# A two-layer attention and feed-forward kernel: the first attention turns its row maxima in two halves of query tiles, and its first step moves its queries in halves

## The reference, cut to what matters

```python
q = _rmsnorm(x @ wq_a.T, q_a_ln_w) @ wq_b.T          # per head 64 plain and 64 rotated columns
ckv, k_pe = split(x @ wkv_a.T)                        # latent of 32, shared rotated key of 64
k_nope, v = split(_rmsnorm(ckv, kv_a_ln_w) @ wkv_b.T)
q_pe, k_pe = _apply_rope(...), _apply_rope(...)       # x * cos + rotate_half(x) * sin
scores = einsum('bqhd,bkhd->bhqk', q_full, k_full) * softmax_scale
scores = where(causal, scores, lowest)
attn = softmax(scores, axis=-1)
out = einsum('bhqk,bkhd->bqhd', attn, v) @ wo.T
```

## Time and profile before

| what | us |
|---|---|
| median of 3 runs (2199.75 to 2222.36) | 2202.95 |
| the profiled execution, its own time | 2218.44 |
| the profiled execution, its span | 2216.7 |
| TensorE busy, share of the span | 2008.4, 91% |
| VectorE, ScalarE, GpSimd busy | 1167.0, 883.8, 480.9 |
| mean granted TensorE clock | 0.933 of full |

### The profile page before, as it was taken

The page is one execution under the profiler, slowest core; times in us unless marked ns, Lnnn a source line. Parts: engine busy times, 40 slices in busy tenths (PEclk is TensorE's granted clock), DMA queues, the critical chain, the costliest instruction groups (busy, mean ns, idle before and its releaser), DMA issues. The chain is left out here.

```text
span 2216.7 us, 34036 instructions
## 1 busy us (share of the span) xinstructions
PE 2008.4 (91%) x12632; PEld 1153.7 (52%) x12632; DVE 1167.0 (53%) x2541; ACT 883.8 (40%) x1861; POOL 480.9 (22%) x376
## 2 busy tenths in 40 slices
PE   5858999999999999999976899996999999999698
PEld 4535666656666656665643454553444444444244
DVE  3536555565555555556401454445676676673166
ACT  3402444444444444444430122221566665665222
POOL 0011444444443434444330000000000000000000
PEclk8867999999999999999997999995899999998699
DMA  9742232222333233322208221126132122211201
GB/s 310 254 136 58 58 78 57 58 60 70 78 78 78 68 78 78 78 55 55 67 23 258 67 67 52 51 93 138 21 51 46 34 49 47 37 30 22 92 29 48
DMA packets 100856, 172.19 MB, mean 78 GB/s; under 512 B 25738, under 2 KB 46378, under 8 KB 100562
## 3 DMA queue, kind: packets, MB, share of 16 engines
q1 hardware_dynamic: 100690, 170.01, 29.2%
HBM read 84.32 MB, written 29.38 MB: 51 GB/s over the span
## 5 line engine op out<-in xcount | busy, mean ns | idle before, releaser
L822 ACT ACTIVATE at_prob<-at_scp 128x512 f32<-128x512 f32 (+1 forms) x608 | 349.6, 575 | 533.1 <-PE at_scp L923 524.5
L856 DVE CUSTOM_DVE_ANT_0 at_junk<-at_mxp,causal 128x128 f32<-128x128 f32 (+3 forms) x512 | 240.5, 486 | 339.6 <-PE at_mxp L932 334.9
L1549 ACT ACTIVATE as_prob<-as_scp 128x512 f32<-128x512 f32 (+2 forms) x640 | 309.6, 563 | 202.2 <-PE as_scp L1645 149.5
L932 PE MATMUL at_mxp<-l_khi,at_qhi 96*128 96x512 f32 (+2 forms) x768 | 262.4, 406 | 24.9 <-DMA at_qhi<-at_shi 21.1
L919 PE MATMUL at_scp<-at_qhi,l_khi 97*128 97x512 f32 (+1 forms) x608 | 260.4, 428 | 8.2 <-issue 4.5
L1599 DVE TENSOR_REDUCE as_mxd<-as_mxp 128x2 f32<-128x256 f32 (+3 forms) x256 | 203.6, 821 | 105.3 <-PE as_mxp L1664 103.4
L922 PE MATMUL at_scp<-at_qlo,l_khi 96*128 96x512 f32 (+1 forms) x608 | 235.0, 387 | 0.0
L923 PE MATMUL at_scp<-at_qhi,l_klo 96*128 96x512 f32 (+1 forms) x608 | 233.6, 384 | 0.0
L1584 POOL TENSOR_TENSOR l_att_t<-l_att_t,as_spread 64x1024 f32<-64x1024 f32 x16 | 37.9, 2368 | 878.9 <-DMA as_spread<-l_recips 878.9
L1642 PE MATMUL as_scp<-as_q,l_keys 49*128 49x512 f32 (+2 forms) x640 | 213.9, 459 | 13.4 <-ACT as_prob L1549 10.8
L1659 PE MATMUL as_mxp<-l_keys,as_q 48*128 48x512 f32 (+2 forms) x768 | 186.9, 467 | 35.7 <-DVE as_mxf L1597 13.9
(11 more groups left out here) (204 smaller groups left out, 2742.1 us busy)
## 6 DMA issues: line engine op xcount, KB each, us to landing
at_qhi<-at_shi SPq DMA_DIRECT2D x192, 128.0 KB, 2.4
at_qlo<-at_slo SPq DMA_DIRECT2D x192, 128.0 KB, 2.4
op_ring<-in_wmod SPq DMA_DIRECT2D x12, 1024.0 KB, 6.2
op_ring<-in_wo_t SPq DMA_DIRECT2D x8, 1024.0 KB, 13.6
at_spread<-l_recips SPq DMA_DIRECT2D x64, 128.0 KB, 2.8
l_o<-at_u_sb SPq DMA_DIRECT2D x16, 512.0 KB, 3.2
ml_o_t<-l_o SPq DMA_DIRECT2D x16, 512.0 KB, 4.2
as_q<-scratch_queries SPq DMA_DIRECT2D x48, 128.0 KB, 4.7
```

The costliest lines, as they stand in the source:

```text
L822: nc.scalar.activation(prob[:, x % RING0, c0:HALF], scp[x % BANKS0][:, c0:HALF], ACT.Exp).then_inc(s["exp_done"], 1)
L856: nc.vector.tensor_tensor_reduce(out=junk[:, u % 2, 0:w], in0=tile[:, 0:w], in1=k.causal[:, HALF - w:HALF], scale=1.0, scalar=LOWEST, op0= ...
L932: nc.tensor.matmul(bank("max", t, u)[:, 0:w], qhi[t % 2][0:KR, j, qt * P:(qt + 1) * P], k.khi[0:KR, t // NG, k0:k0 + w], start=True, stop= ...
L1549: nc.scalar.activation(prob[:, x % RING1, cols], scp[x % BANKS1][:, cols], ACT.Exp).then_inc(s["exp_done"], 1)
```

## The change

1. The maxima of a step are ordered in two halves: first the 16 units of the four lower query tiles of every head (`FIRST_HALF`), then the 32 of the upper tiles. Each half is turned, copied out and moved by itself (`turns`, `row_in`): the lower half of step t + 1 in front of quad 9 of step t, the upper half of step t in front of its own quad 2 (quad 4 in step 0). Quad 0 waits for the lower row (`m_in`), quad 4 for the upper (`m_late`).
2. The units are spread over more quads: 3 + 3 own units in quads 0 and 1, the rest in quads 2 to 11. The projections move from quads 4 to 9 to quads 5 to 10, in step 0 to quads 7 to 10.
3. `qhi` and `qlo` are laid out by halves of the queries, so that each DMA of `queries` writes two runs of 2 KB a row in place of one of 4 KB.
4. The lead-in shrinks to the queries of step 0 and the 16 lower units. The queries of step 0 are moved in halves of 64 KB a DMA (`first_queries`). The upper 32 units of step 0 and the queries of step 1 are made inside step 0, in quads 0 to 3 and 1 to 2.
5. The rotation terms of the second halves of steps 0 and 1 go to `pre`, which is free then, in place of `tm` (`terms`), and the subtraction for the low parts is a call of its own (`low_parts`); in later steps it follows `rotate` at once.
6. In SyncE's queue the upper maxima row of step t stands behind `queries(t+1)`; in step 0 it stands behind `queries(1)` and `queries_low(1)`.

```diff
 QK = [(qc, kt) for qc in range(2) for kt in range(4 * qc + 4)]
-MU = [(j, qt, part) for j in range(G) for qt in range(TILES) for part in range(1 + qt // 4)]
-MAX_AT = {2: 5, 3: 5, 4: 5, 5: 8, 6: 5, 7: 8, 8: 5, 9: 7}
-MID_AT = {3: 3, 5: 3, 7: 3, 9: 3}
-PROJ_AT = {4: 0, 5: 1, 6: 2, 7: 3, 8: 4, 9: 5}
-TURN_AT0 = 11
+MU = [(j, qt, part) for half in range(2) for j in range(G) for qt in range(4 * half, 4 * half + 4) for part in range(1 + half)]
+FIRST_HALF = 4 * G
+OWN_AT = [{0: 8, 1: 8, 2: 8, 3: 8}, {0: 3, 1: 3}]
+MAX_AT = [{6: 8, 7: 8, 8: 7, 9: 7, 10: 6, 11: 6}, {2: 4, 3: 4, 4: 6, 5: 5, 6: 4, 7: 5, 8: 4, 9: 4, 10: 3, 11: 3}]
+MID_AT = {3: 2, 5: 3, 7: 3, 9: 2, 11: 2}
+PROJ_AT = [{7: (0,), 8: (1, 2), 9: (3,), 10: (4, 5)}, {5: (0,), 6: (1,), 7: (2,), 8: (3,), 9: (4,), 10: (5,)}]
+PROJ_FIRST = {1: (0, 1, 2), 2: (3, 4, 5)}
+TURN_A, TURN_B = 9, (4, 2)
 PJ = 6
 SHARE = {2: 2, 3: 4}
 UNITS_OF = [G // SHARE.get(kt - 4 * qc, 1) for qc, kt in QK]
...
 def quad_work(t, n):
 
-    pieces = []
-    if n in PROJ_AT and t + 2 < STEPS0:
-        pieces.append(("queries", t + 2, PROJ_AT[n]))
+
+    later = min(t, 1)
+    pieces = [("queries", 1, u) for u in PROJ_FIRST.get(n, ())] if t == 0 else []
+    if t + 2 < STEPS0:
+        pieces += [("queries", t + 2, u) for u in PROJ_AT[later].get(n, ())]
+    own, ahead = OWN_AT[later], MAX_AT[later]
+    lo = UNITS - sum(own.values()) + sum(own.get(i, 0) for i in range(n))
+    pieces += [("max", t, u) for u in range(lo, lo + own.get(n, 0))]
     if t + 1 < STEPS0:
-        lo = sum(MAX_AT.get(i, 0) for i in range(n))
-        pieces += [("max", t + 1, u) for u in range(lo, lo + MAX_AT.get(n, 0))]
+        lo = sum(ahead.get(i, 0) for i in range(n))
+        pieces += [("max", t + 1, u) for u in range(lo, lo + ahead.get(n, 0))]
     return pieces
 
 
+def queries_ready(t, n):
+
+    later = min(t, 1)
+    done = [(1, u // 3) for u in PROJ_FIRST.get(n - 1, ()) if t == 0 and u % 3 == 2]
+    return done + [(t + 2, u // 3) for u in PROJ_AT[later].get(n - 1, ()) if t + 2 < STEPS0 and u % 3 == 2]
+
+
...
 def lead_in():
 
-    pieces = [("queries", 0, u) for u in range(PJ)]
-    for u in range(UNITS):
-        pieces.append(("max", 0, u))
-        if u + 1 in (UNITS // 4, 5 * UNITS // 8):
-            pieces += [("queries", 1, i) for i in (range(3) if u < UNITS // 2 else range(3, PJ))]
-    return pieces
+    return [("queries", 0, u) for u in range(PJ)] + [("max", 0, u) for u in range(FIRST_HALF)]
+
+
+def turns(t, n):
+
+    return [(t, 1)] * (n == TURN_B[min(t, 1)]) + [(t + 1, 0)] * (n == TURN_A and t + 1 < STEPS0)
 
...
+                def first_queries(hf):
+                    cols = slice(HALF * hf, HALF * (hf + 1))
+                    for blk in range(3):
+                        if blk == 0:
+                            sp.wait_ge(s["lat_hi"], hf + 1)
+                        if blk == 1:
+                            sp.wait_ge(s["qhi_done"], 2 * hf + 2)
+                        for j in range(G):
+                            sp.dma_start(words(qhi[0][LAT * blk:LAT * (blk + 1), hf, j, :]), words(shi[LAT * j:LAT * (j + 1), blk, cols])
+                                         ).then_inc(q_in[0] if hf else s["q_first"], 16)
+
...
+                def queries_low(t):
                     sp.wait_ge(s["lat_lo"], 2 * t + 2)
...
+                def maxima_row(t, half):
+                    sp.wait_ge(s["mrow_done"], 2 * t + half + 1)
+                    sp.dma_start(words(qhi[t % 2][MR:MR + 1, half, :, :]), words(mrow[:, half, :])).then_inc(row_in[half][t % 2], 16)
 
...
-                queries(0)
-                maxima_row(0)
+                for hf in range(2):
+                    first_queries(hf)
+                queries_low(0)
+                maxima_row(0, 0)
                 for t in range(STEPS0):
-                    if t + 1 < STEPS0:
+                    if t == 0:
+                        queries(1)
+                        queries_low(1)
+                        maxima_row(0, 1)
+                    elif t + 1 < STEPS0:
                         queries(t + 1)
+                        maxima_row(t, 1)
+                        queries_low(t + 1)
+                    else:
+                        maxima_row(t, 1)
                     if t >= 2:
                         outcome(t - 2)
                     if t >= 1:
                         results(t - 1)
                     if t + 1 < STEPS0:
-                        maxima_row(t + 1)
+                        maxima_row(t + 1, 0)
                 results(STEPS0 - 1)
                 for t in range(STEPS0 - 2, STEPS0):
                     outcome(t)
...
-                    cols = slice(HALF * hf, HALF * (hf + 1))
+                    tm = terms(n)
                     pool.wait_ge(s["terms_done"], 4 * n + 4)
                     nc.gpsimd.tensor_tensor(tm[:, 0, :], tm[:, 0, :], tm[:, 2, :], ALU.subtract).then_inc(s["rot_done"], 1)
                     nc.gpsimd.tensor_tensor(tm[:, 1, :], tm[:, 1, :], tm[:, 3, :], ALU.add).then_inc(s["rot_done"], 1)
+
+                def low_parts(t, hf):
+                    n = 2 * t + hf
+                    tm = terms(n)
+                    cols = slice(HALF * hf, HALF * (hf + 1))
                     if t >= 1:
...
                     x = t * SCORES + FIRST_UNIT[EARLY[i]]
                     pool.wait_ge(s["exp_done"], x + G)
+                    if i == 1 and t == 0:
+                        pool.wait_ge(s["qlo_done"], 8)
...
-                    for hf in range(2):
-                        rotate(t, hf)
+                for hf in range(2):
+                    rotate(0, hf)
+                for hf in range(2):
+                    low_parts(0, hf)
+                for hf in range(2):
+                    rotate(1, hf)
+                    low_parts(1, hf)
...
                 for t in range(STEPS0):
                     presum(t, 1)
                     if t + 2 < STEPS0:
                         rotate(t + 2, 0)
+                        low_parts(t + 2, 0)
                     presum(t, 2)
                     presum(t, 3)
                     if t >= 1:
                         normalise(t - 1)
                     if t + 2 < STEPS0:
                         rotate(t + 2, 1)
+                        low_parts(t + 2, 1)
                 normalise(STEPS0 - 1)
 
             @block.scalar
...
-                        if t + 2 < STEPS0 and PROJ_AT.get(n - 1, 0) % 3 == 2:
-                            queries_hi(t + 2, PROJ_AT[n - 1] // 3)
+                        for which in queries_ready(t, n):
+                            queries_hi(*which)
                         if n == 2 and t >= 1:
                             copy_out(t - 1, 1)
                         if n == 6:
...
                         dve.wait_ge(s["lat_hi"], n + 1)
                         nc.vector.tensor_tensor(slo[:, 0, cols], pj[:], shi[:, 0, cols].bitcast(F32), ALU.subtract).then_inc(s["lat_lo"], 1)
                     else:
-                        if part == 1 and n >= 1:
-                            dve.wait_ge(s["qlo_done"], 2 * n)
+                        tm = terms(n)
+                        if part == 1 and n >= 2:
+                            dve.wait_ge(s["qlo_done"], 2 * n if n >= 4 else 2 * n - 2)
                         for row, tab in ((0, k.cos_t), (3, k.sin_t)) if part == 1 else ((2, k.sin_t), (1, k.cos_t)):
...
+                def turn_maxima(t, half):
+                    if half == 0:
+                        pe.wait_ge(s["mx_done"], t * UNITS + FIRST_HALF)
+                    else:
+                        pe.wait_ge(s["mx_joined"], t + 1)
+                    freed(pe, "turn", t, half)
+                    nc.tensor.transpose(bank("turn", t, half)[0:G * TILES // 2, 0:P], mxd[:, half].rearrange("p j q -> p (j q)"), k.ident[:]).then_inc(s["mt_ready"], 1)
 
...
-                    if n == TURN_AT0 and t + 1 < STEPS0:
-                        turn_maxima(t + 1)
+                    for which in turns(t, n):
+                        turn_maxima(*which)
                     if n == 0:
                         moved(pe, lo_in, t)
                         pe.wait_ge(m_in[t % 2], 16 * (t // 2 + 1))
+                    if n == 4:
+                        pe.wait_ge(m_late[t % 2], 16 * (t // 2 + 1))
                     pieces = quad_work(t, n)
```

85 lines of the change are left out of this document (42 added, 43 removed).

## The result

| | before | after |
|---|---|---|
| median (runs) | 2209.51 us (4, 2199.75 to 2222.36) | 2338.83 us (4, 2334.93 to 2343.14) |
| span of the profiled execution | 2216.7 us | 2333.2 us |
| TensorE busy, share of the span | 2008.4, 91% | 2021.6, 87% |
| mean granted TensorE clock | 0.933 | 0.916 |

The changed kernel takes 1.058 times as long, with a 95% interval of 1.0548 to 1.0613: slower, as forecast, at 2339 us against a forecast of 2330 us.

A forecast was written before the change was run, and what follows sets the result against it. TensorE, busy 91% of the span, was taken as the bound. Thirteen later steps (+114 us), the first step (+15.5) and steps 14 and 15 (about -3) gave +127 on 2202.95: 2330 us, range 2275 to 2371.

The forecast's parts named there:

- S: In a later step's timeline, the time of its first score, from which the other times are counted.
- idle: Steps 1 to 13, quad 9: TensorE stands idle some 8.7 us before the early sums.
- loss by the clock, a step: Behind the idle stretch TensorE's clock falls to half, costing 1.6 to 3.3 us, taken as 2.5.
- a step: Steps 1 to 13: 66.9 us against 60.6, plus 2.5 for the clock; thirteen steps cost 114 us.
- steps 14 and 15: The last two steps make no queries and keep the gains: about 3 us less.
- The chain: Steps 1 to 13: ScalarE's later copies delay GpSimd's low parts and sums, so early sums start at S + 57.8.
- Rival A: The chain stalls every step but TensorE's clock holds: 2293 us; chance 0.21.
- The first step: Step 0: quad 0 starts at 160.8, quad 4 near 208, early sums near 257; step 1 starts 15.5 us later.
- the 9.1 us behind the sums: Later steps: time from the early sums' start at S + 57.8 to the next step's first score, 9.1 us.
- the upper row's place in SyncE's queue: Later steps: row issued behind `queries(t+1)`, lands near S + 11.5 before quad 4 near S + 16.5; priced at nothing.
- B: Rival: the turn counts, early sums find `pre` ready; a step 58.6 us, 2173 us in all, faster; chance 0.07.
- C: Rival: only the first step loses, by SyncE's queue; later steps gain under 1 us each; 2203 us, no change; chance 0.03.

The follow-up runs named there:

- the one line of it in the kernel before: The kernel before with only its six projections moved from quads 4 to 9 to quads 5 to 10: 2355.65 us, 1.0624 of the kernel before.
- the version with the three edits: Changed kernel with half 0's copies ahead of quad 8's exps, early sums in quad 11, step 0's upper row first in SyncE's queue: 2179.8 us, 0.982 of the kernel before.

## Why the prediction was right

The mechanism was right, and most of its sizes; a few errors offset one another.

| | forecast | measured |
|---|---|---|
| last exp of quad 8 ends | S + 43.6 | S + 44.1 |
| sums on GpSimd end | S + 57.5 | S + 57.8 |
| TensorE asks for them | S + 49.1 | S + 49.9 |
| idle | 8.7 us | 7.86 us |
| loss by the clock, a step | 2.5 us | 2.05 us |
| a step | 66.9 + 2.5 = 69.4 us | 69.42 us |
| quad 0, quad 4 of step 0 | 160.8, near 208 | 161.45, 207.64 |
| early sums of step 0 | near 257 | 254.29 |
| step 1 starts | near 270 (+15.5) | 268.71 (+14.1) |
| steps 14 and 15 | -3 us | about 0 |
| in all | +127 us | +129 us by the medians |

**Where the cost is.** The chain that I read off three engines, copy, low parts, sums, TensorE, is the cause: moving either link of it (the low parts on GpSimd, the copies on ScalarE) takes the loss away, 1.058 to 1.0045 and 1.0029, and the one line of it in the kernel before brings it, 1.062. That eight fewer units in quads 2 to 8 would not let TensorE run ahead by a whole quad was right; with a unit priced at 0.2 us between scores, its arrival came out within 1 us.

**The clock.** 2.5 us a step was taken from two stretches of the kernel before; the run with dummy matmuls gives 2.05. Rival A (2293) would have needed the clock to hold. Its ground, that the waits of up to 1.9 us at the turn left the step at its pace, was not quite so in the trace of before either. Behind two of these waits, each of 1.72 us, the granted clock fell, and those steps lasted 62.62 and 62.82 us where the other ten lasted 60.1 to 61.2. The first of the two, and a stretch behind its wait:

```profile
488.97:551.59 62.62, 60.90 (x367) 37.95 (x366) 35.14 (x95) 26.04 (x47) 27.38 (x22) 0.97 0.28 69
495.60:499.00 3.40, 3.40 (x28) 1.01 (x24) 0.00 (x0) 0.00 (x0) 1.72 (x2) 0.63 0.65 146
```

**The first step.** Both its parts came as forecast, the queue that holds the upper row until 205.55 and the early sums behind the copies of quad 9. Its size was 1.4 us too high: the early sums came 2.7 us sooner than forecast, and from there to step 1 it took 14.4 us, not 13.1.

**What was off.** The term for steps 14 and 15, -3: TensorE's pause behind the attention begins 123.6 us later than before, while the early sums of step 13 already came 121.3 later, and 2 us of clock lay behind those; so the last two steps gained nothing. Opposed to that, the sum was made against one profiled execution: its span and that of after differ by 116.5, with 7.1 of difference in unchanged stages, while the medians differ by 129.3. That the total agrees to 2 us is therefore partly luck. The step of 69.4 is not, but for its last tenths: the clock was put 0.45 us too high, and the 9.1 us behind the sums were 9.3 (661.70 to 671.02 at full clock, in the run with the dummy matmuls).

**What I had at nothing and was not.** I covered the upper row's place in SyncE's queue by saying when the row lands. Its other side, that the low parts of step t+1 are moved only behind it and hold VectorE's next write, costs nothing where the projections stand in quads 5 to 7, but 2.1 us a step in quads 4 to 6 (1.020 against 1.006).

**The other rivals.** B was wrong as a forecast and right on the gain: what the turn and the row are worth shows once the stall is gone. C falls with the steps. I gave B a step of 58.6 us; the version with the three edits has 58.90. That it comes so near is partly luck, since B names the waits at the turn and for the row as the gain, and of the 2.07 us only 1.2 are waits. How the gain is divided among the turn, the row and the spreading of units was not taken apart by runs. Nor was the lead-in's shortening run by itself.
